# First attention of a two-layer transformer: rotary halves exchanged by DMA, projection one step earlier

## The reference

```python
q = (x @ Wq).reshape(B, L, H, DH)
k = (x @ Wk).reshape(B, L, KV, DH)
v = (x @ Wv).reshape(B, L, KV, DH)
cos, sin = (jnp.cos(emb), jnp.sin(emb))
q = q * cos + _rotate_half(q) * sin     # _rotate_half: concat(-t2, t1)
k = k * cos + _rotate_half(k) * sin
attn = jnp.einsum('bqkgd,bskd->bkgqs', qg, k) * scale
attn = jax.nn.softmax(attn, axis=-1)
out = jnp.einsum('bkgqs,bskd->bqkgd', attn, v).reshape(B, L, H * DH)
return out @ Wo
```

## Time and profile before

| | us |
|---|---|
| median of three runs | 1546.24 |
| lowest, highest | 1546.03, 1549.05 |
| profiled execution, whole time | 1553.07 |
| profiled execution, span from first to last instruction | 1551.1 |

### The profile page before, as it was taken

How to read it: one execution, slowest core, us unless ns; L and a number is a source line. 1 busy time by engine, 2 the same in 40 slices (tenths; PEclk the granted TensorE clock), 3 DMA queues, 4 the chain that set the end, 5 groups by cost and what they waited for, 6 DMA issues and landing times. The chain is left out here.

```text
span 1551.1 us, 29838 instructions
## 1 busy us (share of the span) xinstructions
PE 1149.9 (74%) x10864; PEld 718.6 (46%) x10864; DVE 1105.2 (71%) x1557; ACT 608.0 (39%) x1176; POOL 841.0 (54%) x772
## 2 busy tenths in 40 slices
PE   2388999989999899999999436555448886165554
PEld 1135565645655556556565424333214676133343
DVE  2377978868789588797878458986227775469983
ACT  1134545545455354564546123332124330133331
POOL 0267878869788597987979213331026564023320
PEclk9578999999999899999999858988655898668896
DMA  2221212212121121221211000000000000000001
GB/s 69 74 43 43 43 33 53 43 31 49 34 55 37 24 63 33 53 43 22 63 33 33 15 0 1 0 0 1 14 11 1 1 1 1 14 0 0 1 0 55
DMA packets 48100, 42.17 MB, mean 27 GB/s; under 512 B 7734, under 2 KB 46154, under 8 KB 47946
## 3 DMA queue, kind: packets, MB, share of 16 engines
q1 hardware_dynamic: 47946, 40.14, 11.4%
HBM read 6.42 MB, written 2.10 MB: 5 GB/s over the span
## 5 line engine op out<-in xcount | busy, mean ns | idle before, releaser
L661 POOL TENSOR_TENSOR a_p_lo<-a_probs 128x512 f16<-128x512 f32 x384 | 418.6, 1113 | 29.1 <-ACT a_probs L515 25.3
L515 ACT ACTIVATE a_probs<-a_ps_s 128x512 f32<-128x512 f32 x512 | 304.0, 597 | 327.2 <-PE a_ps_s L447 322.7
L597 DVE TENSOR_REDUCE a_nmx<-a_ps_m 128x2 f32<-128x1024 f32 x256 | 311.0, 1216 | 33.4 <-PE a_ps_m L430 32.6
L463 PE MATMUL a_ps_o<-a_v_hi,a_probs 128*128 128x65 f16 x2048 | 243.0, 196 | 7.6 <-POOL a_p_lo L661 7.6
L464 PE MATMUL a_ps_o<-a_v_lo,a_probs 128*128 128x64 f16 x2048 | 240.3, 194 | 0.0
L465 PE MATMUL a_ps_o<-a_v_hi,a_p_lo 128*128 128x65 f16 x2048 | 240.0, 194 | 0.0
L463 PEld LDWEIGHTS a_ps_o<-a_v_hi,a_probs 128*128 128x128 bf16 x2048 | 189.3, 98 | 79.1 <-issue 48.5
L445 PE MATMUL a_ps_s<-a_qq,a_kk 128*128 128x512 f16 x512 | 198.0, 387 | 10.4 <-issue 6.2
L464 PEld LDWEIGHTS a_ps_o<-a_v_lo,a_probs 128*128 128x128 bf16 x2048 | 191.1, 99 | 25.1 <-issue 1.0
L447 PE MATMUL a_ps_s<-a_qq,a_k_l 65*128 65x512 f16 x512 | 198.6, 388 | 0.0
L465 PEld LDWEIGHTS a_ps_o<-a_v_hi,a_p_lo 128*128 128x128 f16 x2048 | 190.9, 98 | 0.0
(11 more groups left out here) (218 smaller groups left out, 2105.9 us busy)
## 6 DMA issues: line engine op xcount, KB each, us to landing
a_qq<-a_rhi SPq DMA_DIRECT2D x128, 128.0 KB, 2.4
a_qq<-a_rlo SPq DMA_DIRECT2D x128, 64.0 KB, 2.1
a_kk<-a_rhi SPq DMA_DIRECT2D x64, 64.0 KB, 2.0
a_k_l<-a_rlo SPq DMA_DIRECT2D x32, 64.0 KB, 2.0
out_x<-x_sb SPq DMA_DIRECT2D x1, 2048.0 KB, 8.7
a_qq<-a_nmT SPq DMA_DIRECT2D x64, 2.0 KB
m_w<-in_wmod SPq DMA_DIRECT2D x2, 384.0 KB
a_probs<-in_wq SPq DMA_DIRECT2D x1, 512.0 KB, 3.7
```

Of the source, the lines that this page charges most:

```text
L463: nc.tensor.matmul(out, hi, v_hi[:, b % 2, kt, g, 0:65], start=(kt == 0), stop=False)
L515: nc.scalar.activation(probs[:, p % 2, kt, h, :], ps_s[:, i % 2, :], ACT.Exp, scale=DH0 ** -0.5).then_inc(exp_done, 1)
L597: nc.vector.tensor_reduce(nmx[:, p % 2, i:2 * QT:QT], ps_m[:, n % 2, :, :], axis=X, op=ALU.max, negate=True).then_inc(free[n % 2], 1)
L661: nc.gpsimd.tensor_tensor(p_lo[:, p % 2, kt, h, :], pr, pr.bitcast(BF16)[:, 1:2 * L:2], ALU.subtract).then_inc(lo_pool, 1)
```

## The change

The weights with exchanged halves are gone: a projection is three matmuls into one bank. VectorE's product reads this bank twice (a broadcast) and writes the cosine and the sine product, the sine table having its sign in the other half. New items RD and KD: SyncE sends the sine product with its 32-row blocks exchanged into a new tile `rsw`, in four DMAs, and GpSimd's sum waits for them. `rcs` and `rsw` have four buffers. In the schedule A moves from step p - 3, slot 1, to step p - 4, slot 6, with RD in slot 7 behind it, while RS, RH and RL stay in slots 3 to 5 of step p - 3. B moves from slots 0, 2, 4, 6 to 1, 3, 5, 7; O from slot 3 to 2. VectorE takes the low parts of tiles 3 and 7 in place of 2 and 6. The K items are spread over two steps.

```diff
@@ pipeline()
-        if pair(s + 2):
-            for i in range(4):
-                slots[2 * i].append(("B", s + 2, i))
+        if pair(s + 4):
+            slots[6].append(("A", s + 4))
+            slots[7].append(("RD", s + 4))
         if pair(s + 3):
-            slots[1].append(("A", s + 3))
             slots[3].append(("RS", s + 3))
             slots[4].append(("RH", s + 3))
             slots[5].append(("RL", s + 3))
+        if pair(s + 2):
+            for i in range(4):
+                slots[2 * i + 1].append(("B", s + 2, i))
...
         if pair(s - 2):
-            slots[3].append(("O", s - 2))
+            slots[2].append(("O", s - 2))
...
         if (b := seq(-5)) is not None:
             for m in range(2):
                 slots[2 + 3 * m].append(("K", b, m))
-                slots[4 + 2 * m].append(("KS", b, m))
-                slots[5 + 2 * m].append(("KH", b, m))
-                slots[6 + m].append(("KL", b, m))
+                slots[3 + 3 * m].append(("KD", b, m))
+            slots[7].append(("KS", b, 0))
         if (b := seq(-4)) is not None:
+            slots[0].append(("KH", b, 0))
+            slots[1].append(("KL", b, 0))
+            slots[1].append(("KS", b, 1))
+            slots[2].append(("KH", b, 1))
+            slots[3].insert(0, ("KL", b, 1))
             slots[5].append(("V", b))
@@ tiles and the split of the low parts
-        rcs = sb("rcs", [128, 2, 2, L])
+        rcs = sb("rcs", [128, NR, 2, L])
+        rsw = sb("rsw", [128, NR, L])
...
-        LO_DVE, LO_POOL = (2, 6), (0, 1, 3, 4, 5, 7)
+        LO_DVE, LO_POOL = (3, 7), (0, 1, 2, 4, 5, 6)
@@ SyncE
-                if kind == "RL":
+                if kind in ("RD", "KD"):
+                    key = it[1:]
+                    r = rope[key]
+                    t.jobs(free, job[("A" if kind == "RD" else "K",) + key], 1)
+                    for k in range(4):
+                        src, dst = slice(32 * k, 32 * (k + 1)), slice(32 * (k ^ 1), 32 * (k ^ 1) + 32)
+                        sp.dma_start(rsw[dst, r % NR, :], rcs[src, r % NR, 1, :]).then_inc(rope_swap[r % NR], 16)
+                elif kind == "RL":
@@ TensorE
-                    for swap in range(2):
-                        out = ps_m[:, n % 2, swap, :]
-                        hi, lo = (w[:, swap, j * 128:(j + 1) * 128] for w in (w_hi, w_lo))
-                        nc.tensor.matmul(out, hi, hT_hi[:, b % 2, :], start=True, stop=False)
-                        nc.tensor.matmul(out, hi, hT_lo[:, b % 2, :], start=False, stop=False)
-                        last = nc.tensor.matmul(out, lo, hT_hi[:, b % 2, :], start=False, stop=True)
+                    hi, lo = (w[:, j * 128:(j + 1) * 128] for w in (w_hi, w_lo))
+                    nc.tensor.matmul(bank, hi, hT_hi[:, b % 2, :], start=True, stop=False)
+                    nc.tensor.matmul(bank, hi, hT_lo[:, b % 2, :], start=False, stop=False)
+                    last = nc.tensor.matmul(bank, lo, hT_hi[:, b % 2, :], start=False, stop=True)
@@ VectorE
-            for w, heads in ((wq_hi, H0), (wq_lo, H0), (wk_hi, KV0), (wk_lo, KV0)):
-                w4 = w[:].rearrange("p s (h a c) -> p s h a c", h=heads, a=2)
-                for a in range(2):
-                    last = nc.vector.tensor_copy(w4[:, 1, :, a, :], w4[:, 0, :, 1 - a, :])
-            last.then_inc(swapped, 1)
...
-                    t.ropes(rope_sum, r - 1, 1)
-                    nc.vector.tensor_tensor(rcs[:, r % 2, :, :], ps_m[:, n % 2, :, :], cossin[:],
+                    t.ropes(rope_sum, r - NR + 1, 1)
+                    nc.vector.tensor_tensor(rcs[:, r % NR, :, :], ps_m[:, n % 2, 0:1, :].to_broadcast([128, 2, L]), cossin[:],
                                             ALU.mult).then_inc(free[n % 2], 1)
@@ GpSimd
-                    t.jobs(free, job[("A" if kind == "RS" else "K",) + key], 1)
+                    t.wait(rope_swap[r % NR], (r // NR + 1) * 64, ROPE16 // NR * 64)
                     t.ropes(rope_lo, r - 1, 1)
-                    nc.gpsimd.tensor_tensor(rot[:, r % 2, :], rcs[:, r % 2, 0, :], rcs[:, r % 2, 1, :],
+                    nc.gpsimd.tensor_tensor(rot[:, r % 2, :], rcs[:, r % NR, 0, :], rsw[:, r % NR, :],
                                             ALU.add).then_inc(rope_sum, 1)
```

More of the change, by code:

```diff
@@ L201, in layer0_attention @@
     ROPE16 = rope[(LOOP_FROM + 3 + PERIOD,)] - rope[(LOOP_FROM + 3,)]
-    assert JOBS16 % 2 == 0 and ROPE16 % 2 == 0
+    assert JOBS16 % 2 == 0 and ROPE16 % NR == 0
     with ExitStack() as ex:
@@ L212, in sem @@
             return ex.enter_context(nc.semaphore(f"a0_{name}"))
[L215 to L218, removed]
+        wq_hi = sb("wq_hi", [D, H0 * DH0], FP16)
+        wq_lo = sb("wq_lo", [D, H0 * DH0], FP16)
+        wk_hi = sb("wk_hi", [D, KV0 * DH0], FP16)
+        wk_lo = sb("wk_lo", [D, KV0 * DH0], FP16)
         wv_hi = sb("wv_hi", [D, KV0 * DH0], FP16)
@@ L265, in layer0_attention @@
         loaded, ready = sem("loaded"), sem("ready")
-        swapped, w_hi_done = sem("swapped"), sem("whi")
+        split, w_hi_done = sem("split"), sem("whi")
+        rope_swap = [sem(f"rswap{k}") for k in range(NR)]
         full = [sem("full0"), sem("full1")]
@@ L387, in _ @@
             pe.wait_ge(ready, 5)
-            pe.wait_ge(swapped, 1)
+            pe.wait_ge(split, 1)
             def item(t, it):
@@ L487, in _ @@
             nc.scalar.activation(ident16[:], ident[:], ACT.Copy).then_inc(ready, 1)
-            for whole, hi in ((wq, wq_hi[:, 0, :]), (wk, wk_hi[:, 0, :]), (wv, wv_hi[:])):
+            for whole, hi in ((wq, wq_hi[:]), (wk, wk_hi[:]), (wv, wv_hi[:])):
                 nc.scalar.activation(hi, whole, ACT.Copy, scale=WSCALE).then_inc(w_hi_done, 1)
@@ L547, in _ @@
             dve.wait_ge(w_hi_done, 3)
-            for whole, hi, lo in ((wq, wq_hi[:, 0, :], wq_lo[:, 0, :]), (wk, wk_hi[:, 0, :], wk_lo[:, 0, :]),
-                                  (wv, wv_hi[:], wv_lo[:])):
-                nc.vector.scalar_tensor_tensor(out=lo, in0=whole, scalar=WSCALE, in1=hi, op0=ALU.mult,
-                                               op1=ALU.subtract)
-            nc.vector.drain()
-            for w, heads in ((wq_hi, H0), (wq_lo, H0), (wk_hi, KV0), (wk_lo, KV0)):
-                w4 = w[:].rearrange("p s (h a c) -> p s h a c", h=heads, a=2)
-                for a in range(2):
-                    last = nc.vector.tensor_copy(w4[:, 1, :, a, :], w4[:, 0, :, 1 - a, :])
-            last.then_inc(swapped, 1)
+            for whole, hi, lo in ((wq, wq_hi[:], wq_lo[:]), (wk, wk_hi[:], wk_lo[:]), (wv, wv_hi[:], wv_lo[:])):
+                last = nc.vector.scalar_tensor_tensor(out=lo, in0=whole, scalar=WSCALE, in1=hi, op0=ALU.mult,
+                                                      op1=ALU.subtract)
+            last.then_inc(split, 1)
             def item(t, it):
@@ L1549, in tables @@
     sin = np.sin(emb).T.astype(np.float32) / np.float32(WSCALE)
-    sin[:DH0 // 2] *= -1
+    sin[DH0 // 2:] *= -1
     sin = np.tile(sin, (2, 1))
```

## The result

The changed kernel takes 1599.76 us, the median of four runs (1594.78 to 1601.17), against 1546.93 us for the kernel before (four runs, 1546.03 to 1549.05) on the same chip. The ratio is 1.0334, 95% interval 1.0308 to 1.036: 3.3% slower. The forecast was 1571 us, slower, with a range up to 1597, and 1599.76 lies above that range. The side came out as drawn and so did the ring of waits in the plain steps; the size was too small, by 20.6 us on the profiled execution (45.6 us against 25).

A forecast was written before the change was run, and what follows sets the result against it. TensorE bounds the kernel before; after the change a ring of waits through GpSimd, SyncE's queue and DMAs would. Start +12 and seven sequences +13 give +25 us, 1578 profiled, 1571 after the 6.8 us offset to the median; range 1530 to 1597.

The forecast's parts named there:

- ring of waits: First attention's plain steps: waits through GpSimd, SyncE's queue and the exchange DMAs close a loop that sets each step's time.
- The bare sum of 10.22 us: One round in a plain step, sum to sum, without slow issues; bounds 9.45 to 10.6 us.
- slow issues: SyncE DMA issues over 0.9 us, 28 of 416 before; each costs 0.9 us, 0.48 us per round.
- L2: GpSimd's low part that the new split puts between its sum and the rotated rows' low part; 1.00 us per round.
- T: Time of a plain step of the first attention with slow issues included: 10.7 us against 10.12.
- The K steps: Steps with K and V projections: SyncE's queue in series, 30.4 us to the next-but-one sum against 30.9 before, gaining 0.5.
- The output-projection step: Step with the output projection has room for the exchange and gains 0.65 us from fewer matmuls.
- The start: Before the first scores: K exchanges and K rows queue ahead of the first query exchange on SyncE; 11.7 us later.
- The sum: Net per sequence +1.9 us, for seven sequences +13 us; with the start's +12, +25 us in all.
- rival 1: Exchange hidden in the first attention, TensorE decides: 8 us less per sequence, 1498 us in all; chance 0.12.
- Rival 2: Waits in the first attention as drawn, but slow issues fall outside the round: 1546 us; chance 0.16.
- Rival 3: SyncE's queue worse than counted: landing 2.4 us, slow issues 0.8 us, plain steps 11.4 us, 1600 us; chance 0.10.

The follow-up runs named there:

- e1: Changed kernel with SyncE's query-row DMAs listed behind the exchange DMAs instead of ahead of them; 1538.5 us.
- e4: Changed kernel without the exchange DMAs, GpSimd adding the two products as they stand (rotation left incomplete); 1512.4 us.
- e2: Changed kernel with two exchange DMAs of 64 rows instead of four of 32, same bytes (computes another rotation); 1538.1 us.
- e8: Changed kernel with each exchange DMA cut into two of 256 columns, same bytes; 1755.4 us.
- e10: e4 with the second K half's sum, copy and low part moved later, as in e6 (rotation incomplete); 1485.6 us.
- e6: Changed kernel with the second K half's sum, copy and low part moved behind the queries' sum, exchange left as it was; 1584.3 us.
- e5: e1 with the second K half's sum, copy and low part also moved later, as in e6; 1528.0 us.
- e9: e5 with SyncE's K-row DMAs as later items of their own and the V step's query rows moved to the next step; 1515.1 us.
- e3: Changed kernel with the old split of low parts, VectorE taking tiles 2 and 6 again; 1594.6 us.
- e7: Changed kernel with the four exchange DMAs issued from ScalarE's queue instead of SyncE's; 1637.9 us.

## Why the prediction missed

- *The ring is real and decides the plain steps:* right. e1 cuts it by order alone and e4 by leaving the exchange out; both give 9.4 us per plain step. e2 and e8 change only the number of issues for the same bytes: 9.7 and 13.4 us. ScalarE, the maxima and the projection 2.2 us after the sum are as described.
- *Its size:* **a term that failed.** The bare sum of 10.22 us holds: the shortest of the 28 rounds is 10.08. Their mean is 11.11, and the 1.03 above the shortest are, by part: 0.45 in SyncE's issues (the forecast's slow issues, 0.48; they are as frequent as forecast, 40 of 736 over 0.9 us, mean 1.44, and 28 of 416 before); 0.22 in GpSimd's low part L2, which takes up to 1.49 us instead of 1.04 in 14 of the 28; and 0.35 between the last issue of the exchange and the sum, 2.10 us in 18 rounds and 2.37 to 4.14 in the other ten, with GpSimd idle. The forecast has no term for the last two; they are 0.57 us a round. T was 10.7 and is 11.16 per plain step: 1.8 us per sequence.
- *The K steps:* **the larger step that failed.** It put them at 36.65 us with the next step, slow issues included, 0.25 more than before; they take 39.6, 3.0 above the forecast (the kernel before averages 0.7 above the one sequence I used, so 2.3 of it is the change's). It said that RS comes 4.0 us after the K step's start, "less what the long step before gives back", and that RL is ready at 7.5. In the sequence of step 43 the K step starts at 663.05 and the sum at 668.98: 5.9 us. The W step gives nothing back: GpSimd waits there for VectorE's `a_yg` (until 653.85, below) and only then takes the low parts and the sum, at 657.34. From there all is late: the query rows' issues start at 9.8 (7.5), and the maxima go out at 26.0 (23.1). And I counted SyncE's queue alone: GpSimd's second K half ahead of the queries' sum was taken as a gain ("spread GpSimd's K work"), while it holds the fp16 copy, the maxima and TensorE's V. GpSimd in the W and the V step, ScalarE, then TensorE in the V step of the changed kernel:

```profile
653.85 1.53 POOL L673 TENSOR_TENSOR x_sb<-x_sb,a_yg 128x512 f32 x1 [6.67 <-DVE a_yg L627]
...
680.27 1.26 POOL L651 TENSOR_TENSOR a_rot<-a_rcs,a_rsw 128x512 f32<-128x512 f32 x1 [0.66 <-DMA a_rsw<-a_rcs]
...
682.49 1.15 POOL L656 TENSOR_TENSOR a_rlo<-a_rot,a_rhi 128x512 f16<-128x512 f32 x1
683.60 1.71 POOL L651 TENSOR_TENSOR a_rot<-a_rcs,a_rsw 128x512 f32<-128x512 f32 x1
```

```profile
685.34 0.63 ACT L534 ACTIVATE a_rhi<-a_rot 128x512 f16<-128x512 f32 x1 [2.10 <-POOL a_rot L651]
```

```profile
686.18 0.40 PE L429 MATMUL a_ps_m<-a_wv_hi,a_hT_hi 128*128 128x256 f16 x1 [1.97 <-ACT a_nmT L545]
...
692.66 0.39 PE L458 MATMUL a_ps_s<-a_qq,a_kk 128*128 128x512 f16 x1 [0.51 <-DMA a_qq<-a_nmT]
```

The queries' sum is the one at 683.60. V waits until 686.18, and the next scores for the maxima's DMA until 692.66: both causes stand in one step, each for itself. e4 (V step 14.6 to 16.7 us without any exchange) and e10 (11.9 to 12.0) show that the first is GpSimd's order. With the exchange in it the same move gives less: e6's K, V, next is 1.1 us under the change, e5's 2.6 under e1. The forecast also took the clock as 1.00 in the attention. In the changed kernel it stood at 0.50 for part of every one of the seven V steps, in the kernel before in none, and over the seven sequences for 78.5 us instead of 20.5 (e4: 41.0, e10: 13.7, e8: 221.9). What that costs the change was not taken apart.
- *The output-projection step:* forecast 0.65 us shorter, measured 1.3 shorter on average.
- *The start:* right, to 0.35 us. SyncE's queue is two exchanges of K, twelve issues of K rows, then the first exchange of queries. GpSimd's first sums of queries:

```profile
79.39 1.26 POOL L651 TENSOR_TENSOR a_rot<-a_rcs,a_rsw 128x512 f32<-128x512 f32 x1 [8.51 <-DMA a_rsw<-a_rcs]
...
89.25 1.26 POOL L651 TENSOR_TENSOR a_rot<-a_rcs,a_rsw 128x512 f32<-128x512 f32 x1 [6.71 <-DMA a_rsw<-a_rcs]
...
99.09 1.26 POOL L651 TENSOR_TENSOR a_rot<-a_rcs,a_rsw 128x512 f32<-128x512 f32 x1 [6.68 <-DMA a_rsw<-a_rcs]
```

  Forecast 78.9 and 98.8, rounds of 9.9: measured 79.39 and 99.09, rounds of 9.86 and 9.84. First scores 12.05 us later, forecast 11.7.
- *The sum:* per sequence 5.4 us instead of 1.9; the 3.5 are 2.3 from the K steps and 1.8 from the ring's size, less 0.7 in W. Times seven: 24 us, of which 4 are given back outside the sequences.
- *Rivals:* rival 1's 1498 us supposed an exchange that is hidden everywhere; without any exchange the kernel takes 1512.4, so it left out the K items too (with them moved, 1485.6). Rival 2 fell: the slow issues cost 0.45 us of a round. Rival 3's time (1600) came true in part by luck: the exchange lands in 2.0 us in the median, not 2.4, though its late landings are there (up to 4.14 us from the last issue to the sum), and 2.5 us per sequence stand in the K steps, which it had not drawn so.
- The rule of the Trainium skill (DMA: Bandwidth & Descriptors, Rules for kernel authors) to issue the DMA early, compute, and wait on its semaphore late would have given rival 1. The traces agree with it only where the item is early in the queue that issues it: e1 moves RD ahead of four waiting DMAs and gains 61 us. The Trainium skill also says (DMA: Bandwidth & Descriptors, Issuing engines are not separate DMA queues) that initiating a DMA is usually small beside the DMA. The traces don't agree here: four issues in a row hold SyncE 2.48 us in the median, the landing of one is 2.0, and e2 and e8 follow the count of issues.

Open: why the slow issues come at fixed places, why some exchanges land late, and what makes up the 29.5 us between e9 and e10; the rest of the exchange's cost was not taken apart.

## What to carry to other kernels

When work moves to a DMA, look at what stands ahead of it in the issuing queue and what that waits for: a short transfer listed behind a DMA that waits for the last round closes a ring, and the ring's length is the step's. Count issues, not bytes (here with DMAs of 32 to 128 KB), and on a GpSimd or ScalarE that is half idle on average still ask what is queued behind each moved item. An item that is moved for balance is judged by the wait it puts on its successor in the same queue; and when one is taken out (e3), look at which item moves up into its place.

## What the runs showed of the hardware

- An exchange of 128 KB (e2) landed 2.3 us after its issue in the median, one of 64 KB 2.0 (the change), one of 32 KB 1.9 (e8): nearly no price for size. Four issues in a row hold SyncE 2.48 us (the change), ScalarE 2.47 (e7), in the median.
- Not every transfer lands alike: from the last issue of an exchange to the sum that waits for it are 2.10 us in 18 of 28 rounds and 2.37 to 4.14 in ten.
- VectorE reads one PSUM bank twice in one instruction at the price of two banks: 1.22 us.
- GpSimd's low part of the exponentials takes 1.04 us (in 319 of 384 in the changed kernel, to 1.15) or mostly 1.49 (65). All 65 long ones lay 0.4 us or more beside VectorE's own operation of the same kind (L611); of the short ones 25 did, so that alone does not decide it.
- Where TensorE stalled in the V step its granted clock fell to the lower level for a stretch: mean 0.79 in one V step of e4 and 0.88 in one of e9, against 1.00 in e10's; TensorE was busy 13.49, 12.69 and 11.01 us there for nearly the same matmuls. A V step of e4 without such a stretch has 11.14 us of busy time and takes 14.60 us instead of 16.5.
